# The softplus correction of channel tiles 2 and 3 moves from GpSimd to VectorE

## The reference, cut to what matters

```python
dt = jax.nn.softplus(dt @ dt_proj_w + dt_proj_b)
A = -jnp.exp(A_log)
dA = jnp.exp(dt[..., None] * A)
dBu = (dt * u)[..., None] * Bm[:, :, None, :]
def step(s, inp):
    dA_t, dBu_t, C_t = inp
    s = dA_t * s + dBu_t
    y = jnp.einsum('bdn,bn->bd', s, C_t)
    return (s, y)
```

## Time and profile before

| | us |
|---|---|
| median of 3 runs | 3019.35 |
| lowest and highest | 3016.56, 3025.76 |
| span of the profiled execution, first to last instruction | 2958.7 |
| median of the runs above that span | 60.65 |

### The profile page before, as it was taken

One profiled execution on the slowest core, in us unless ns is written; L12 is line 12 of the kernel. 1 busy time (PEld: TensorE's weight loads), 2 busy tenths in 40 slices (PEclk: granted clock), 3 DMA queues, 4 the chain that ended last, 5 costly groups with the idle time before them and its releaser, 6 DMA issues. The chain is left out here.

```text
span 2958.7 us, 36517 instructions
## 1 busy us (share of the span) xinstructions
PE 2351.0 (79%) x12305; PEld 1420.5 (48%) x12305; DVE 2163.5 (73%) x3017; ACT 1383.5 (47%) x2217; POOL 575.3 (19%) x569
## 2 busy tenths in 40 slices
PE   4448896889778977887788869787879688988991
PEld 2335354535453545444544545345535453556880
DVE  4993898489948894899669975998589852246666
ACT  5323654366535663566356634654465424143440
POOL 4000101120131013111311120212120230025661
PEclk8558897899889987998799979998999789988995
DMA  2320231023201321133113311231033182355757
GB/s 105 120 79 8 103 113 57 15 87 128 74 28 60 128 94 35 42 126 107 42 35 109 117 49 42 92 127 56 8 112 121 60 212 97 103 195 174 219 180 302
DMA packets 136229, 292.85 MB, mean 99 GB/s; under 512 B 14288, under 2 KB 79200, under 8 KB 135792
## 3 DMA queue, kind: packets, MB, share of 16 engines
q1 hardware_dynamic: 122224, 251.96, 26.2%
q0 software_dynamic: 13824, 38.55, 3.6%
HBM read 220.91 MB, written 69.54 MB: 98 GB/s over the span
## 5 line engine op out<-in xcount | busy, mean ns | idle before, releaser
L1367 DVE TENSOR_TENSOR_SCAN scan<-scan 128x1024 f32<-128x1024 f32 x256 | 585.9, 2289 | 34.4 <-ACT scan L1097 26.4
L2047 PE MATMUL bank<-ident,scan 128*128 128x128 f32 x2048 | 325.3, 315 | 168.9 <-DVE scan L1376 158.1
L1097 ACT ACTIVATE scan<-scan 128x511 f32<-128x511 f32 x512 | 337.2, 713 | 164.2 <-DVE scan L1367 163.5
L2047 PEld LDWEIGHTS bank<-ident,scan 128*128 128x128 f32 x2048 | 271.6, 162 | 260.1 <-DVE scan L1376 158.4
L1399 DVE TENSOR_TENSOR scan<-scan 128x1024 f32<-128x1024 f32 x256 | 310.5, 1213 | 29.5 <-PE bank L2047 28.5
L1376 DVE TENSOR_TENSOR scan<-scan 128x1024 f32<-128x1024 f32 x256 | 312.0, 1219 | 7.8 <-DVE rest L1579 7.5
L1936 PE MATMUL bank<-hT,wslot 128*128 128x512 f32 x512 | 246.9, 607 | 0.0
L1541 DVE TENSOR_REDUCE rest<-bank 128x2 f32<-128x1024 f32 (+3 forms) x176 | 196.5, 1126 | 66.5 <-PE bank L2118 63.5
L819 POOL DMA_INDIRECT rows_dram<-stage,slot_at x128 | 164.9, 1288 | 370.4 <-DVE scan L1367 313.1
L1144 ACT ACTIVATE rest<-bank 128x2048 f32<-128x2048 f32 (+3 forms) x128 | 158.2, 1236 | 146.7 <-PE bank L2138 146.6
L1936 PE MATMUL bank<-xT,scan 128*128 128x512 f32 (+1 forms) x352 | 185.0, 672 | 7.4 <-ACT xT L983 4.8
(11 more groups left out here) (341 smaller groups left out, 4231.2 us busy)
## 6 DMA issues: line engine op xcount, KB each, us to landing
scan<-bc_dram SPq DMA_DIRECT2D x256, 512.0 KB, 3.8
wslot<-wt SPq DMA_DIRECT2D x64, 384.0 KB, 3.5
rows_dram<-pad SPq DMA_DIRECT2D x32, 670.0 KB
scan<-y_dram SPq DMA_DIRECT2D x32, 512.0 KB, 10.1
rest<-rows_dram SPq DMA_DIRECT2D x108, 134.0 KB, 2.5
scan<-rows_dram SPq DMA_DIRECT2D x52, 134.0 KB, 2.7
scan<-wt SPq DMA_DIRECT2D x4, 1536.0 KB, 13.6
xa<-x SPq DMA_DIRECT2D x8, 512.0 KB, 3.8
```

The source lines that it names most:

```text
L1097: i = a.activation(decay[:, unit % 2, n, 1:], dt[:, c, 1:], ACT.Exp, scale=a_neg[:, c, 2 * pair + n:2 * pair + n + 1])
L1367: d.tensor_tensor_scan(flat, decay[:, unit % 2].rearrange("p n t -> p (n t)"), flat, 0.0, ALU.mult, ALU.add).then_inc(decay_used.sem, 1)
L2047: m = t_.matmul(A.bank(("yT", c))[:, t * P:(t + 1) * P], drive[:, unit % NDRIVE, n, t * P:(t + 1) * P], ident[:, :], is_transpose=True, st ...
```

## The change

The three GpSimd instructions for each of tiles 2 and 3 go, and with them ScalarE's step that subtracts 1. VectorE makes the correction of all four tiles in the same way. The place of the calls for tiles 2 and 3 is as before: ahead of units 10 and 11. The decay of units 16 and 17 waits for VectorE's dt instead of GpSimd's.

```diff
@@ GpSimd, scan_part
                 for c in range(2, NCT):
                     yield
-                    pool.wait_ge(sa.sem, sa.named(turn, f"sp_log{c}"))
-                    apart(pool)
-                    s = sp_.step(g.tensor_tensor(dtu[:, c], sp_exp[c], dtu[:, c], ALU.subtract).then_inc(sp_.sem, 1))
-                    pool.wait_ge(sp_.sem, sp_.at(turn, s))
-                    s = sp_.step(g.tensor_tensor(dtu[:, c], sp_log[c], dtu[:, c], ALU.add).then_inc(sp_.sem, 1))
-                    pool.wait_ge(sp_.sem, sp_.at(turn, s))
-                    marked(f"dt{c}", sp_.step(g.tensor_tensor(dt[:, c], dt[:, c], dtu[:, c], ALU.add).then_inc(sp_.sem, 1)))
                 yield from late_part(late, turn)
@@ ScalarE, scan_part
-                    s = sa.step(a.activation(dtu[:, c], sp_exp[c], ACT.Identity, bias=1.0).then_inc(sa.sem, 1))
-                    if c >= 2:
-                        act.wait_ge(sa.sem, sa.at(turn, s))
-                        sa.step(a.activation(dtu[:, c], dtu[:, c], ACT.Copy, bias=-1.0).then_inc(sa.sem, 1))
+                    sa.step(a.activation(dtu[:, c], sp_exp[c], ACT.Identity, bias=1.0).then_inc(sa.sem, 1))
                     marked(f"sp_log{c}", sa.step(a.activation(sp_log[c], sp_exp[c], ACT.Ln, bias=1.0).then_inc(sa.sem, 1)))
@@ ScalarE, decay_unit
                 if unit % (2 * NPAIR) < 2:
-                    ready = sv if c < 2 else sp_
-                    act.wait_ge(ready.sem, ready.named(turn, f"dt{c}"))
+                    act.wait_ge(sv.sem, sv.named(turn, f"dt{c}"))
@@ VectorE, dtu_of
                 def dtu_of(c):
-                    if c < 2:
...
-                    else:
-                        dve.wait_ge(sp_.sem, sp_.named(turn, f"dt{c}"))
+                    dve.wait_ge(sa.sem, sa.named(turn, f"sp_log{c}"))
+                    s = sv.step(d.scalar_tensor_tensor(dtu[:, c], dtu[:, c], 1.0, sp_exp[c], ALU.subtract, ALU.subtract).then_inc(sv.sem, 1))
+                    dve.wait_ge(sv.sem, sv.at(turn, s))
+                    s = sv.step(d.tensor_tensor(dtu[:, c], sp_log[c], dtu[:, c], ALU.subtract).then_inc(sv.sem, 1))
+                    dve.wait_ge(sv.sem, sv.at(turn, s))
+                    s = marked(f"dt{c}", sv.step(d.tensor_tensor(dt[:, c], dt[:, c], dtu[:, c], ALU.add).then_inc(sv.sem, 1)))
+                    dve.wait_ge(sv.sem, sv.at(turn, s))
                     marked(f"dtu{c}", sv.step(d.tensor_tensor(dtu[:, c], dt[:, c], u[:, c], ALU.mult).then_inc(sv.sem, 1)))
```

## The result

| | before | after |
|---|---|---|
| median of 4 runs, us | 3022.56 | 3053.99 |
| lowest and highest, us | 3016.56, 3031.03 | 3043.99, 3062.58 |
| ratio after to before, 95% interval | | 1.0097, 1.0068 to 1.0127 |

The change costs 31.4 us. The forecast was 3023 with a range of 3006 to 3043, and the time lies above the range. Of the rivals the second is nearest: it gave 3043 to 3048 and turn starts 310.6 us apart.

A forecast was written before the change was run, and what follows sets the result against it. VectorE (73% busy) and TensorE (79%) were taken to bound the turns, both without gaps in the MLP. Per turn -2.0 + 4.3 = +2.3 us, damped to 3.3 once: 2962.0 plus 60.65 gives 3023, range 3006 to 3043.

The forecast's parts named there:

- The 4.3 reach line 1513 nearly whole: MLP stage: six added VectorE instructions, 4.3 us, delay the sum of line 1513 by nearly all of it; bounds 2.4 to 4.3.
- stage (b): Attention, back and forth between TensorE and ScalarE; claimed to end 2.0 us earlier per turn, bounds 0 and 3.9.
- Rival 3: Shorter pause before the first score unit lets TensorE keep or sooner regain its clock; 3.6 us a turn, 3009; chance 0.15.
- the distance stays 307.19: Turn starts: a push of 2.3 us in every turn moves the turns by at most 3.3 us once, distance unchanged.
- the factor of 0.3: Between turns: a turn passes on some 0.3 of a deviation, read from excesses of 0.41, 0.12 and 0.0 us.
- The pair of rows: TensorE transposes, eight and sixteen each in 1.97 us; taken to show late work meets the faster clock, halving a delay.
- Rival 1: Not damped: +2.3 us comes every turn, +14.5 us in all, giving 3034; chance 0.18.
- Rival 2: Slower by more: later clock rise, or lost attention gain with nothing damped; 3043 to 3048; chance 0.17.
- first form: Behind line 1513's sum, the clock rises a stretch later; 3.4 us a turn, 24 in all, giving 3043.
- second form: The 2.0 us at the attention's head are lost and nothing is damped; 28.5 us in all, giving 3048.
- No DMA is moved.: DMA queues: the change was taken to move no load, so no cost was counted there.
- the 60.65 us "around the span": Execution's own time outside the span, median minus profiled span; added to 2962.0 to give 3022.65.

The follow-up runs named there:

- e2: Kernel before, GpSimd's part kept, plus six VectorE instructions of the change's forms with unread results ahead of units 10 and 11; ratio to before 1.0085.
- f4: Kernel after with the correction and log term of tile 3 left out, so half the addition; one execution, 2998.26 us beside 2967.23 for before.
- e1: Kernel after with the correction and log term of tiles 2 and 3 left out, so GpSimd's part gone and nothing added; ratio to before 0.9972.
- e3: Kernel after with the corrections and products by u of tiles 2 and 3 ahead of units 4 and 5 instead of 10 and 11; ratio to before 1.0003.
- g3: e3 plus 5 unread TensorE matmuls in the wait ahead of the first score unit; 2948.38 us against 2967.48 for before, ratio 0.9938.
- h1: Kernel after plus 5 unread TensorE matmuls in the wait ahead of the first score unit; ratio to before 1.0022.
- h3: e1 plus 5 unread TensorE matmuls in the wait ahead of the first score unit; ratio to before 0.993.
- h2: Kernel before plus 8 unread TensorE matmuls in the wait ahead of the first score unit; ratio to before 1.0056.
- g1: Kernel after with SyncE's order edited so MLP weight tile 3 loads ahead of unit 12's B row; ratio to before 1.0118.
- g2: Kernel before with SyncE's order edited so one more broadcast load goes ahead of weight tiles 3 and 4; ratio to before 1.0161.
- f1: Kernel before plus unread matmuls in TensorE's four long waits of a turn; ratio to before 1.0114.

## Why the prediction was wrong

**Right: what the change does to each engine.** The steps stretched by GpSimd take 0.69 us; the pause is 3.48 (3.4 forecast); the additions stand at 0.72 and take 4.3. In turn 0 the scan and drives have their full speed again, as the timeline of VectorE after shows (compare):

```profile
64.84 1.22 DVE L1383 TENSOR_TENSOR scan<-scan 128x1024 f32<-128x1024 f32 x1
66.10 2.29 DVE L1351 TENSOR_TENSOR_SCAN scan<-scan 128x1024 f32<-128x1024 f32 x1
68.31 1.20 DVE L1383 TENSOR_TENSOR scan<-scan 128x1024 f32<-128x1024 f32 x1
```

The 2.0 us are as the rows gave them. How the two engines held each other up is seen in turn 0 of before, in GpSimd's timeline beside VectorE's:

```profile
66.31 2.12 POOL L845 TENSOR_TENSOR scan<-scan 128x512 f32<-128x512 f32 x1
68.50 3.12 POOL L847 TENSOR_TENSOR scan<-scan 128x512 f32<-128x512 f32 x1
```

VectorE's drive ends at 67.31, and GpSimd's instruction 1.12 us later (68.43). VectorE's scan, started at 67.34, ends 2.14 us after that (70.57), about its length alone. GpSimd's next ends 1.05 us after the scan (71.62), and VectorE's second drive 1.10 us after that (72.72). So they took turns, each standing until the other had ended. The Trainium skill (SBUF — State Buffer, Who interferes with whom) says that the loser of the shared port blocks fully. The trace agrees: by these ends, GpSimd's 1.59 us beside a correction step hold about 0.5 us of its own waiting (an estimate), and VectorE lost the other 1.1 less an overlap of 0.15, which is the 0.95. The prediction read the 1.59 as work, and so took that rule to give 3.2 us at the start.

**Right, a little large: the MLP.** "The 4.3 reach line 1513 nearly whole" with a lower bound of 2.4: they are 3.7 in after and in e2, and 1.5 of 2.16 in f4. The slack was 0.7 us and not the 1.9 that TensorE's row showed.

**Wrong, first: "So stage (b) ends 2.0 us earlier."** The 2.0 us are won and 1.9 lost, in after, e1 and e3 alike. The bound of 0 was in the text; the value was chosen by the size of the pause. What takes them is TensorE's clock: the back and forth between TensorE and ScalarE meets a second short low stretch. After's own turns show it (53.0 us with two, 51.5 with one, 50.1 with none), and the runs show it by opposites: with the clock held across the pause the attention takes 49.8 to 49.9 (g3, h1, h3) instead of 53.0. The hold without the gain (h2) shortens nothing, but its filler overran, so whether a well-sized hold alone would shorten the kernel before stays open. Rival 3 had this price (3.6 us a turn, 3009 as the time) but not what it hangs on: a shorter pause alone doesn't keep the clock.

**Wrong, second: "the distance stays 307.19", the factor of 0.3.** This is the step that decided the miss. It was read from the first two distances, 307.60 and 307.31, that is from a single disturbance that dies out. A delay that comes in every turn is not cut to a part: after's usual turn has 175.5 us up to line 1513's sum, before 171.9, and the difference of 3.5 is in the distance nearly whole (3.45).

What "rest" does give back are small deviations, and those whole. before, e1, e3, h1 and h2 reach the sum after 171.8 to 172.3 us, "rest" takes 135.4 to 134.9, and the distance is 307.20 in each. after, e2 and g1 reach it after 175.5, 175.7 and 175.9 us, "rest" takes 135.2, 135.0 and 134.8, and the distance is 310.65. So the distance is neither damped by a factor nor passed on as it is, but held to values 3.4 apart; the prediction's rows, in which 0.41 and 0.12 us die out, showed only the first half. The pair of rows behind it (8 transposes in 1.97 us at one place, 16 in 1.97 at another) shows that the clock has two levels (the eight ran behind the gap, where a window has 0.50), not that a late turn meets the higher one.

It can also be worse than passed on. With a delay of 1.6 us (g2) "rest" is 5.3 longer, mainly because the low stretch behind line 1513's sum lasts longer (a group of products in 3.78 us instead of 1.99). After has one "rest" of 142.7, where the last stage of the linear attention has slid into a low stretch (1.11 us a group instead of 0.65). In f4's turn of 320.9, with a "rest" of 147.6, both happen. So the profiled execution's 31.3 us are not six times 3.45: four distances carry 3.45, one 10.1 and the first 7.4. The first may not be the change's, since two executions of the kernel before differ by 13.8 there. Why after slides in turn 4, which reaches line 1513's sum in 174.6 us, and not in turn 5, which needs 175.5, stays open, as does what spaces the distances.

**Rivals.** Rival 1 (undamped) was nearer in its rule, with the wrong terms: 7 x (-2.0 + 4.3) where -0.2 + 3.7 was right. Rival 2's last sentence, "the 2.0 at stage (b)'s head are lost and nothing is damped", is what happened: it gave 3048, with 4.3 for the additions. Its first form, a clock that rises a stretch later behind line 1513's sum, gave 310.6 as the distance. TensorE's rows tell the two apart: in after's usual turn the products behind the sum come as early (780.08 - 762.10 = 17.98 us, before 1074.72 - 1056.68 = 18.04) and as fast (1.98 and 1.99 us) as before, so its 3.45 us lie ahead of the sum and the second form holds. The first form is what g2 and f4 show, at an MLP only 1.5 to 1.6 us longer.

**Wrong, third: "No DMA is moved."** None is moved in SyncE's order, but four loads wait for VectorE and the weights stand behind them, so all come 4.1 us later. It would have been a new bound: TensorE waits 16.1 us in seven. g1 takes it away and the usual turn stays at 310.65, with VectorE as late as before that edit; no share of it in the 31 us is seen, but the step was too short.

**Wrong, fourth: the 60.65 us "around the span".** They don't exist: the spans lie about 2 us below their execution's time (3041.9 and 3043.99; 2970.9 and 2972.7). The profiled execution of before simply was faster than the timed runs. The h runs show of what kind this is: h1 starts the maxima of `rest_part(7)` at 2424.1 and e3 at 2425.9, yet their spans are 3030.2 and 2962.3. The 68 us between them lie behind that, where the expert blocks are. The change doesn't make them: that last stage up to the updates takes 63.8 us in after, 73.0 in h2, on the kernel before, and 41 in before and in g1, which has the change. That happened to shift nothing in the forecast, since it went back to the median.

## What to carry to other kernels

Cut each turn of a periodic kernel into stages by marks on one engine, and see which stage takes what another gave; a disturbance that dies out says nothing of one that comes in every turn. Put added work to the stage where its engine waits anyway (units 4 and 5: nothing, units 9 to 11: 3.5 us a turn), and if a pause of TensorE gets shorter, check whether its clock is still low behind it: here the usual turns got shorter only where the pause was both shorter and held (0.9938 and 0.993).

## What was unexpected in the hardware

- Turn distances take few values: 303.79, 307.20, 310.65 and 314.05 us are steady ones, 3.4 apart, and 317.3 and 320.7 occur too; f4 and the kernels with four fillers have some in between. Very different kernels share a value (before, e1, e3, h1, h2), and an MLP 1.5 to 1.6 us longer (f4, g2) moves a turn by 0, 3.4, 6.8 or 13.6. What spaces them so is not shown.
- A short low stretch of TensorE's clock (3.0 and 3.2 us at 0.50) comes while TensorE is busy for all of it, and costs the attention some 1.5 us; in g3, with the long one gone, one at 667 to 671 is left, and after's turn 7 has none.
- VectorE and GpSimd, each with both operands in the buffer "scan", took strict turns: a scan of 2.29 us alone took 3.23, and GpSimd's step beside it 3.12.
- More clock is not less time: f1 has a mean of 0.908 against 0.868 and takes 1.14% longer than before.
- Two executions of one kernel can differ by 13.8 us in one turn (307.4 and 321.2) and be equal in all others.
